# Ten runs of zero products on TensorE made longer in a chain of graph and feed-forward layers

## The reference

```
x = x + L0_gnn(norm(x))    graph attention, 8 heads, then 1 head
x = x + L0_ffn(norm(x))    6 gated class tokens, the rest a 96-wide GELU layer
x = x + L1_gnn(norm(x))    graph attention, 8 heads, then 1 head
x = x + L1_ffn(norm(x))    relu(x W1) W2 Wo, then a layer norm
x = x + L2_gnn(norm(x))    graph convolution with W
x = x + L2_ffn(norm(x))    8 experts, the best one: silu(x w1) * (x w2), then w3
x = x + L3_gnn(norm(x))    34 relations with a 768x768 matrix each, then a convolution
x = x + L3_ffn(norm(x))    8 experts, the best two, then a layer norm
```

## Time and profile before

| | |
|---|---|
| median of 3 runs | 1392.44 us (1392.18 to 1395.44) |
| profiled execution | 1392.8 us, span 1391.0 us, mean granted clock 0.981 |
| TensorE (PE) | 1305.9 us busy, 94% of the span, 7833 products |
| weight loads on TensorE (PEld) | 1148.3 us, 83% |
| DVE | 1003.6 us, 72% |
| ScalarE (ACT) | 627.3 us, 45% |
| GpSimd (POOL) | 216.9 us, 16% |

### The profile page before, as it was taken

How to read it: one execution, slowest core, us unless ns; L and a number is a source line. 1 busy time by engine, 2 the same in 40 slices (tenths; PEclk the granted TensorE clock), 3 DMA queues, 4 the chain that set the end, 5 groups by cost and what they waited for, 6 DMA issues and landing times.

```text
span 1391.0 us, 21373 instructions
## 1 busy us (share of the span) xinstructions
PE 1305.9 (94%) x7833; PEld 1148.3 (83%) x7833; DVE 1003.6 (72%) x1677; ACT 627.3 (45%) x795; POOL 216.9 (16%) x160
## 2 busy tenths in 40 slices
PE   5799999987899999987898999999999999999986
PEld 4499999964699999967677888988889888988875
DVE  7888888977788888975847756665666556655564
ACT  2266665645456656544335334333433343334331
POOL 0024444341033444440000000000000000002000
PEclk9999999998999999998989999999999999999998
DMA  9466556653366556543334544454445444543520
GB/s 346 152 189 213 167 167 208 191 144 93 99 202 199 166 170 216 180 121 118 121 103 159 212 166 151 161 195 171 151 156 195 176 151 152 191 177 128 184 72 23
DMA packets 103718, 227.32 MB, mean 163 GB/s; under 512 B 16688, under 2 KB 34672, under 8 KB 103684
## 3 DMA queue, kind: packets, MB, share of 16 engines
q1 hardware_dynamic: 72780, 192.43, 39.4%
q10 hardware_dynamic: 20968, 31.78, 7.9%
q0 software_dynamic: 9936, 2.66, 2.0%
HBM read 216.56 MB, written 10.29 MB: 163 GB/s over the span
## 4 chain that ended last, share of the span: by engine, by line
PE 81%; DVE 12%; ACT 2%; DMA 2%; issue 2%; DVEq 0%; ACTq 0%; SPq 0%
PE bank L418 80%; DVE w_lo L1181 3%; DVE stats L1219 1%; ACT w_hi L892 1%; DMA w_in<-L_gnn_W 1%; PE bank L457 1%; DVE h_lo L1181 1%; DVE spare L1394 1%; DVE a_bc L1394 1%; DVE x_sb L1181 1%; PE bank L514 1%; DMA w_in<-L_gnn_W_root 1%; DVE xT_lo L1181 1%; DVE neg_b L1184 0%; DMA x_sb<-x 0%
## 5 line engine op out<-in xcount | busy, mean ns | idle before, releaser
L1181 DVE TENSOR_TENSOR w_lo<-w_in,w_hi 128x2304 fp32r<-128x2304 f32 (+4 forms) x162 | 396.5, 2477 | 61.0 <-ACT w_hi L892 60.7
L892 ACT ACTIVATE w_hi<-w_in 128x2304 fp32r<-128x2304 f32 (+4 forms) x162 | 328.1, 2062 | 224.4 <-PE bank L418 197.2
L418 PE MATMUL bank<-w_hi,xT_hi 128*128 128x384 f32 (+3 forms) x942 | 324.7, 345 | 6.9 <-DVE xT_lo L1181 4.5
L418 PE MATMUL bank<-w_lo,xT_hi 128*128 128x384 f32 (+3 forms) x942 | 310.1, 341 | 0.0
L418 PE MATMUL bank<-w_hi,hid_hi 128*128 128x512 f32 (+2 forms) x858 | 293.9, 342 | 5.8 <-DVE hid_lo L1181 3.5
L418 PE MATMUL bank<-w_lo,hid_hi 128*128 128x512 f32 (+2 forms) x858 | 271.6, 337 | 0.0
L418 PE MATMUL bank<-w_hi,xT_lo 128*128 128x384 f32 (+3 forms) x942 | 248.0, 342 | 0.0
L418 PE MATMUL bank<-w_hi,hid_lo 128*128 128x512 f32 (+2 forms) x858 | 224.6, 339 | 0.0
L418 PEld LDWEIGHTS bank<-w_hi,xT_hi 128*128 128x128 f32 (+1 forms) x942 | 179.1, 190 | 36.3 <-issue 8.2
L418 PEld LDWEIGHTS bank<-w_hi,hid_hi 128*128 128x128 f32 (+1 forms) x858 | 161.8, 189 | 42.3 <-issue 5.3
L418 PEld LDWEIGHTS bank<-w_lo,xT_hi 128*128 128x128 f32 (+1 forms) x942 | 179.2, 190 | 13.6
(11 more groups left out here) (225 smaller groups left out, 1565.7 us busy)
## 6 DMA issues: line engine op xcount, KB each, us to landing
w_in<-L_gnn_W_rel SPq DMA_DIRECT2D x68, 1152.0 KB, 5.9
w_in<-L_gnn_W SPq DMA_DIRECT2D x66, 1152.0 KB, 6.2
table<-zrow SPq DMA_DIRECT2D x1, 9216.0 KB, 36.2
scores_b<-table ACTq DMA_DIRECT2D x34, 256.0 KB, 3.0
a_bc<-L_gnn_a_src ACTq DMA_DIRECT2D x18, 384.0 KB, 3.6
a_bc<-L_gnn_a_dst ACTq DMA_DIRECT2D x18, 384.0 KB, 5.0
key_row<-key_rows ACTq DMA_DIRECT2D x16, 256.0 KB, 5.2
w_in<-ffn_out SPq DMA_DIRECT2D x4, 864.0 KB, 7.7
```

The source lines that it names most:

```text
L418: return pe.matmul(out, lhsT, rhs, start=start, stop=stop, **kw)
L892: act.activation(out, ps, func, **kw).then_inc(mark, 1)
L1181: return dve.tensor_tensor(out, a, b, op)
```

## The change

Ten runs of zero products get longer, 54 products in all: 8 + 4 ahead of and between the transposes at the start of L1_ffn, 8 and 6 ahead of the transposes of gcn(0)'s two tiles, 5 ahead of the aggregation in both convolutions, 4 ahead of the gated layer, 6 ahead of the relation layer, 4 ahead of gcn(1) and 4 ahead of L3_ffn. Nothing else differs; the other engines' instructions are the same.

```diff
--- before.py
+++ after.py
@@ -466,7 +466,7 @@
                     if m == 1 and k == 0:
                         pe.wait_ge(ln_low, 4 * i + 4)
                     if m == 0 and k == 4 and i > 0:
-                        turn_tile(i, 1)
+                        turn_tile(i, 1, 6 if i == 4 else 0)
                 return ready
 
             def of_both(i):
@@ -688,8 +688,8 @@
             gat(1)
 
 
-            turn_tile(3, 0, 4)
-            idle(2, 2)
+            turn_tile(3, 0, 12)
+            idle(2, 6)
             turn_tile(3, 1)
 
             def columns(count, half, hi, lo, ks, first_bank, marks, ready):
@@ -719,7 +719,7 @@
                 nodes(1, NODE_BANKS, node_tile(xT_hi, xT_lo, 1, K), of_w(half), of_tile(i, 1)).then_inc(w_used, 1)
                 pe.wait_ge(e_cntT_low, 1)
                 for sm in range(M):
-                    idle(AGG_BANKS[1][0][0], 0 if sm else 2)
+                    idle(AGG_BANKS[1][0][0], 0 if sm else 7)
                     pe.wait_ge(g_low, 2 * s + sm + 1)
                     for m in range(M):
                         last = mm3([(bank[b][:, c0:c1], of_h(sm, o, o + c1 - c0)) for (b, c0, c1, o) in AGG_BANKS[m]],
@@ -737,10 +737,10 @@
                 last.then_inc(f_mm[s], 1)
 
 
-            gcn(0, 1, C_GCN2, 4, 3)
-
-
-            turn_tile(5, 0, 8)
+            gcn(0, 1, C_GCN2, 4, 11)
+
+
+            turn_tile(5, 0, 12)
             idle(6, 2)
 
             def gated(m, half, ready):
@@ -775,7 +775,7 @@
 
 
             pe.wait_ge(x_rows, 1)
-            turn_tile(6, 0, 3)
+            turn_tile(6, 0, 9)
             idle(4, 2)
             def product(m, lhs, half, ready=lambda k: None):
 
@@ -833,10 +833,10 @@
             weights(REL + nth(C_REL))
             pe.wait_ge(r_acc, REL * 2 + 1)
             product(0, node_tile(*REL_T[0], 0, K), 0).then_inc(w_used, 1)
-            gcn(1, 1, C_GCN3, 7, 2)
-
-
-            turn_tile(8, 0, 8)
+            gcn(1, 1, C_GCN3, 7, 6)
+
+
+            turn_tile(8, 0, 12)
             idle(6, 2)
             chunk(C_FFN3)
             nodes(0, NODE_BANKS, node_tile(xT_hi, xT_lo, 0, K), of_w(0), of_tile(8, 0)).then_inc(f_mm[3], 1)
```

## The result

The kernel after takes 1388.88 us (median of 20 runs, 1386.09 to 1393.29), the kernel before on the same chip 1392.53 (20 runs, 1389.52 to 1395.47). By the medians that is 3.65 us less, 1.7 us above the predicted 1387.2 and inside the range. The ratio is 0.9972, 0.28% less, with an interval of 0.9963 to 0.9981 (2.6 to 5.2 us). The gain is clear of the noise, and by a hair within the 0.3% that I had called no change.

What follows compares the result with a forecast made beforehand. The prediction took TensorE, 81% of the span in the chain that ended last, as the bound. Its terms, -2.9 - 0.1 + 0 + 0.4 - 1.7 + 0 - 0.9 = -5.2 us, gave 1387.6, or 1387.2 against the median; range 1383.5 to 1390.8.

Steps and rivals of the forecast that it cites:

- gcn(0)'s first tile: Run of 3 to 11 zeros: hidden, fall at 680.2 goes, but DVE's neg_b sets the time; -0.1 us, between 0 and -0.3.
- step 3: gcn(0)'s second tile, 0 to 6 zeros: hidden; fall taken to stay, 60 to 40, at 0; if gone, 1.7 us less.
- The aggregation in gcn(0): 2 to 7 zeros, not at a wait: +0.4 us, between 0 and +1.1; the same five in gcn(1) are free.
- step 7: Falls at 724.6 and 1345.8 in the router's products, which may move: -0.9 us, bounds +0.5 and -2.9.
- The rival that hung on the rule: Clock kept only at L1_ffn's start, other falls stay, nothing won at the routers: 1390.2 us, median 1389.8; chance 0.24.
- step 5: Start of L2_ffn, turn_tile(5, 0), 8 to 12 zeros: hidden, fall at 710.9 goes; -1.7 us, between 0 and -1.7.
- The three hidden runs: turn_tile(6, 0) 3 to 9, gcn(1)'s first tile 2 to 6, turn_tile(8, 0) 8 to 12: hidden, no falls there, 0.
- its own signs: Wrong if a fall remains or appears behind lengthened runs, hidden zeros outlast their DVE row, or the 660.92 transfer eats L1_ffn's gain.
- step 1: Start of L1_ffn, 4 to 12 and 2 to 6 zeros: hidden, clock stays up; -2.9 us, bounds 0 and -5.0.
- the one in which all three falls go: The fall at gcn(0)'s second tile goes too: another -1.7 us, 1385.5; chance 0.25.

Runs made afterwards that it cites:

- e3: The kernel after with 22 instead of 7 zero products ahead of the aggregation in both convolutions: 1393.52 us, ratio 1.0005 to the kernel before.
- e2: The kernel before with all ten runs of zero products that the change lengthened taken out: 1397.67 us, ratio 1.0032.
- e4: The kernel after with the router's 8-column products spread among the dense products around them: 1388.93 us, ratio 0.9972 to the kernel before.
- e7: The kernel after with the run ahead of gcn(0)'s aggregation back at 2 and the router's products spread among dense ones: 1384.57 us, ratio 0.9948 to the kernel before.
- e1: The kernel before with only the two runs at the start of L1_ffn longer (4 to 12, 2 to 6): 1392.04 us, ratio 0.9994.
- e9: The kernel after with the two runs at the start of L1_ffn back at 4 and 2: 1389.13 us, ratio 0.9968 to the kernel before.
- e11: The kernel before with only the run at turn_tile(5, 0), the start of L2_ffn, longer (8 to 12): 1392.33 us, ratio 0.9999.
- e8: The kernel before with only the six zero products ahead of the transposes of gcn(0)'s second tile: 1391.23 us, ratio 0.9989.
- e13: The kernel before with only the run ahead of gcn(1)'s aggregation longer (2 to 7): 1390.19 us, ratio 0.9983.
- e10: The kernel before, unchanged, profiled and timed again as a control: 1392.84 us, ratio 0.9992.
- e5: The kernel after with the run ahead of gcn(0)'s aggregation back at 2, 7 staying in gcn(1): 1387.83 us, ratio 0.9958 to the kernel before.
- e14: The same kernel as e5, timed again: 1388.94 us, ratio 0.9972 to the kernel before.

## Why the prediction was right or wrong

The same places over the traces, in us between the starts of two rows; the start of L1_ffn counts from the transposes at the end of the attention to the product of L1_ffn that waits for hid_lo (654.11 in the trace of before), the other rows from transposes to transposes, or from the aggregation's first product, or to the end of the span. "Few" is the code of before at that place, "more" that of after; in gcn(1) e3 with its 22 zeros counts as more.

```
stretch                          few                       more
L1_ffn start, no long fall ahead 28.87 28.88 28.51         25.97 25.98
L1_ffn start, fall ahead of it   27.16 27.00 27.28         27.46 27.48 27.48 27.55 27.65
gcn(0) tile 1 to L2_ffn          19.76 19.81 19.76 19.76   18.46 18.43 18.45 (7 zeros ahead of
                                 19.81, e2 19.76           aggregation), 18.21 in four (2)
gcn(1) aggregation to L3_ffn     7.88 9.43 9.42 9.42 9.41  7.89 7.96 7.88 7.87 7.87 7.89 7.87 7.89
                                 e2 7.85
fall at the gated layer's start  2 of 5                    0 of 8
fall at the relation's start     1 of 6                    3 of 7
L2_ffn to relation layer         43.04 42.80 (gated fall   40.52 42.02 41.93 42.02 40.40
                                 too) 41.26 41.28 41.24    (e4 39.86, e7 39.90)
                                 40.46
relation layer to gcn(1)         557.40 with its fall,     557.36 557.37 557.32 with,
                                 555.78 to 555.84 without  555.79 to 555.81 without
L3_ffn to the end, by the zeros  57.65 57.69 57.65 57.47   56.05 57.62 56.38 56.03 56.07 57.72
in gcn(1)                        57.66                     (e4 57.75, e7 55.96)
```

That zeros in a wait hold the clock, at no cost while the wait covers them, was right, and so are the direction and the range. Most of the sizes were not:

1. The start of L1_ffn, put at -2.9. Where no long fall stands ahead, it is worth that: 28.87 with a fall behind the wait, 25.97 with none at all. But in 8 of the 13 executions the fall came earlier, among the attention's last products, and then 12 and 6 zeros cost some 0.4 instead (means 27.15 and 27.52). The mean over the executions is 27.95 without and 27.08 with: -0.9. Taken on to L2_gnn's transposes the means are 53.15 and 52.21, the same 0.9, so the transfer that the earlier trace rows shows doesn't eat it. The time of e1 (-0.8) agrees; that of e9 can't tell. I had read the place of the fall from one execution and taken it for a property of the program.
2. gcn(0)'s first tile, -0.1: the reason was right, and the size nearly. The fall stood there in 3 of 6 executions with 3 zeros (9.53 and twice 9.93 us to the second tile's transposes) and in none of seven with 11 (9.34 to 9.40): -0.2. The time is set by DVE's neg_b of the second tile, whose wait was still 1.84 us behind the six zeros. Where the fall of tile 0 was absent this wait had grown, as step 3 said. In e11:

```profile
688.62 0.88 PE L457 MATMUL bank<-ident,neg_b 128*128 128x128 f32 x6 [3.14 <-DVE neg_b L1184]
```

3. gcn(0)'s second tile: called 60 to 40 to stay. It went in every execution that has the six zeros, and it stood in every one without them: 19.76 to 18.21, which is -1.6 and agrees with e8's time. My argument put 2.1 us of remaining idleness next to a wait of 2.34 and counted the zeros as nothing beside it. What remained was 1.84 us with six zeros ahead of it, and no fall followed.
4. The aggregation in gcn(0): put at +0.4, measured +0.25; e3 confirms that each zero there costs its 0.213. In gcn(1) "free" was right and "nothing won" was wrong. One row of 1.81 us without a fall was the exception: four of the five executions with 2 zeros had a fall behind it, and none of eight with 7 or 22. That is 1.5 us in 4 of 5 cases, -1.2; e13's time says -2.4, with an interval of -0.8 to -3.8 that holds it, and also what step 7 adds below.
5. The gated layer's start: put at -1.7. The fall stood there in 2 of 5 executions with 8 zeros, and between the transposes of L2_ffn's two tiles it cost 1.56 us (6.23 before, 4.67 in e10): -0.6 in the mean; e11 alone measured nothing. With 12 zeros there was none in eight. So the forecast took the cost of one execution for that of all. What I had set against the rule of the Trainium skill that transposes don't count as activity in the way of a matmul ("TensorE: Matmul & The Clock Gate", "Part 4: PE-mode transpose") was misread. In the trace of before a fall stands right behind the sixteen transposes of the earlier trace rows, 1.8 us after the end of the second wait, about as far as the fall of 710.9 stands behind the end of its own wait at 709.01. The row of before:

```profile
1366.40:1369.80 3.40, 3.40 (x12) 2.91 (x12) 0.00 (x0) 0.00 (x0) 0.00 (x0) 0.52 0.00 0
```

Thirteen of the fourteen traces have such a fall, 0.3 to 1.8 us behind that wait. So that row doesn't speak against the rule, and the stretch after at L2_ffn (0.80 us of idleness, six transposes, 0.51 us, no fall) doesn't settle it either: no run here takes transposes out or puts them in. The rival that hung on the rule, in which the fall of step 5 stays, did not come.
6. The three hidden runs, at 0: the zeros themselves cost nothing, waits of 1.26, 0.70 and 0.80 us are left behind them. But at the relation layer 9 zeros did not keep the clock better than 3 (falls in 3 of 7 and in 1 of 6), and such a fall costs 1.5 us (557.4 against 555.8): +0.4 by these shares, which may be chance.
7. The router's falls, -0.9: of about that size in sum, but not where I had put it. Most of the first fall I had counted as covered by the transfer, and it was not. At the first router they stayed, of 3.4 to 6.8 us, in all executions where its products stand together; without the 1.56 of the gated fall the means of the stretch are 41.2 and 41.4, so +0.2. That a fall there costs time is seen beside e4 and e7, which have none: 0.6 us for one of 3.4, 1.4 to 2.1 for one of 6.8. In L3_ffn one of 6.8 stood in four of five executions with 2 zeros in gcn(1) and in two of six with more; to the end it is 57.6 and 56.6 in the mean: -1.0. With so few executions this too may be chance.

The terms as measured: -0.9, -0.2, -1.6, +0.25 and -1.2, -0.6, +0.4, -0.8. That makes some -4.7 us, against the measured -3.65 (means: -3.9); it lies inside the interval of 2.6 to 5.2, and one execution more or less with a fall moves a term by 0.2 to 0.5. The forecast of -5.2 was near it by luck, because opposite errors cancelled: steps 1, 5 and 6 gave 2.0, 1.1 and 0.4 us less than forecast, steps 3 and 4 together 3.0 us more. By its own signs the prediction was wrong in two details: behind the relation layer's run of nine a new fall stood in three of seven executions (e3, e5, e14), and the zeros of step 1 outlasted neg_b by 0.48 us. Of the rivals, the one in which all three falls go was right on gcn(0) and the gated layer, and shares the mis-sized steps 1 and 5.

Not settled: what makes the fall ahead of L1_ffn come early or late in an execution, whether the changed shares of falls at the relation layer and at L3_ffn's router are the change's doing, and why e7 gains what e4 alone does not.

## What to carry to other kernels

A fall of the clock that one trace shows has no fixed place: price it by the share of executions in which it stands there, times what it costs on the path. Filler products in a wait are nearly free, but size them below the shortest wait that occurs there, since they outlast it when something ahead moves; where no wait covers them, each costs its whole time beyond the nearest slack. Ask of each fall what starts later by it, and follow the chain: the first router's fall of 6.8 us held up DVE's gate arithmetic and with it the next transfer by 2.1 us, although that transfer seemed to cover it.

## What the runs showed of the hardware that was not expected

With the same code at that place, the clock fell behind a wait of 1.8 us in gcn(1) in four of five executions, and not in the fifth. In e2, without any zeros, the wait was 2.36 us and no fall followed: the length of the wait alone doesn't decide. With 7 zeros a wait of 0.72 to 0.74 us was left, and no fall followed in any of seven. TensorE's timeline of e13:

```profile
1323.68 0.50 PE L418 MATMUL bank<-h_hi,cntT_hi 128*128 128x512 f32 x1 [0.72 <-DVE h_lo L1181]
```

A fall can also stand where no edit explains it: the one at the relation layer's start (751.8 in e5, 751.1 in e14) is in e3 and e11 too, and not in the kernel after, e4, e7 or e9. The clock of the whole run is the better witness: 0.982 for the kernel before, 0.987 after, 0.991 for e7, in the order of their times (though not for e4: 0.989 at the time of the kernel after).
